# Cross attention and mixture of experts on one core: the mask bias of the scores moved from the score matmuls into the folded key matrix

## The reference, cut to what matters

```python
q = (x @ Wq)...; k = (mem_keys @ Wk)...; v = (mem_values @ Wv)...      # 16 heads of 64
scores = einsum('bhtd,bhsd->bhts', q * inv_temp, k) / sqrt(D)
scores = where(mem_mask, scores, -inf)
# keep the 32 largest of 64 scores of each row and head, softmax over these
out = einsum('bhts,bhsd->bhtd', attn, v) @ Wo
```

## Time and profile before

| what | us |
|---|---|
| median of 3 runs | 1403.3 (1400.73 to 1408.4) |
| the profiled execution | 1396.75 |
| its span, first to last instruction | 1394.9 |
| TensorE busy in the span | 1283.2 (92%) |
| VectorE busy | 942.8 (68%) |
| ScalarE busy | 854.2 (61%) |
| GpSimd busy | 682.3 (49%) |
| mean granted TensorE clock | 0.971 of full |

### The profile page before, as it was taken

How to read it: one execution, slowest core, us unless ns; L and a number is a source line. 1 busy time by engine, 2 the same in 40 slices (tenths; PEclk the granted TensorE clock), 3 DMA queues, 4 the chain that set the end, 5 groups by cost and what they waited for, 6 DMA issues and landing times. The chain is left out here.

```text
span 1394.9 us, 27066 instructions
## 1 busy us (share of the span) xinstructions
PE 1283.2 (92%) x7138; PEld 922.0 (66%) x7138; DVE 942.8 (68%) x6185; ACT 854.2 (61%) x2061; POOL 682.3 (49%) x816
## 2 busy tenths in 40 slices
PE   7868799999999999999999999999972899999996
PEld 5445576577576566656757666655531799989996
DVE  3887987996997998799699789944426122222221
ACT  2334488697878879779787887977860122222221
POOL 2557453555356355445624734632013466666673
PEclk9989999999999999999999999999995899999998
DMA  5210641743363184175337417418513264385551
GB/s 189 83 62 9 167 93 31 169 99 77 101 154 82 55 181 93 40 154 121 77 91 155 91 33 196 78 49 195 93 46 136 77 221 152 82 303 187 188 193 26
DMA packets 105009, 161.43 MB, mean 116 GB/s; under 512 B 35058, under 2 KB 58232, under 8 KB 100760
## 3 DMA queue, kind: packets, MB, share of 16 engines
q1 hardware_dynamic: 86760, 106.51, 32.7%
q0 software_dynamic: 18096, 53.19, 11.7%
HBM read 161.81 MB, written 46.53 MB: 149 GB/s over the span
## 5 line engine op out<-in xcount | busy, mean ns | idle before, releaser
L1013 ACT ACTIVATE pt<-fr 128x512 f32<-128x512 f32 x512 | 277.1, 617 | 25.7 <-PE fr L613 22.6
L1244 DVE CUSTOM_DVE_ANT_0 over<-fr,over 128x256 f32<-128x256 f32 x512 | 197.8, 418 | 86.7 <-ACT over L1023 79.2
L1023 ACT ACTIVATE over<-fr 128x256 f32<-128x256 f32 x512 | 179.0, 391 | 53.4 <-PE fr L613 49.0
L613 PE MATMUL fr<-qs,ks 128*128 128x512 f32 x512 | 189.1, 452 | 3.8 <-DMA qs<-cT 1.3
L613 PE MATMUL fr<-ks,qs 128*128 128x256 f32 x512 | 170.7, 352 | 8.1 <-DVE nmax L1244 3.9
L1358 POOL TENSOR_TENSOR m<-m,e 128x1024 f32<-128x1024 f32 x32 | 75.9, 2371 | 185.0 <-DVE m L1180 185.0
L613 PEld LDWEIGHTS fr<-qs,ks 128*128 128x128 f32 x512 | 87.1, 188 | 86.5 <-issue 50.5
L613 PE MATMUL fr<-kd,qs 128*128 128x256 f32 x512 | 137.5, 283 | 0.0
L814 PE MATMUL ob<-pt,v 128*32 128x512 f32 x1024 | 136.4, 604 | 0.6 <-ACT pt L1013 0.5
L613 PEld LDWEIGHTS fr<-ks,qs 128*128 128x128 f32 x512 | 97.8, 191 | 43.9 <-DVE nmax L1244 25.0
L613 PE MATMUL xs<-VW,pT 128*128 128x256 f32 x512 | 120.2, 389 | 1.8 <-issue 1.7
(11 more groups left out here) (211 smaller groups left out, 2903.9 us busy)
## 6 DMA issues: line engine op xcount, KB each, us to landing
parts_d<-parts SPq DMA_DIRECT2D x32, 512.0 KB, 4.2
ks<-parts_d SPq DMA_DIRECT2D x128, 128.0 KB, 4.0
qs<-parts_d SPq DMA_DIRECT2D x128, 128.0 KB, 4.3
xy_d<-xy SPq DMA_DIRECT2D x32, 256.0 KB, 3.9
kd<-diff_d SPq DMA_DIRECT2D x128, 64.0 KB, 4.1
xyf<-xy_d SPq DMA_DIRECT2D x32, 256.0 KB, 4.0
rows_d<-row SPq DMA_DIRECT2D x32, 256.0 KB, 3.3
diff_d<-diff SPq DMA_DIRECT2D x16, 256.0 KB, 2.3
```

Of the source, the lines that this page charges most:

```text
L613: return pe.matmul(o, l, r, start=first, stop=last)
L1013: act.activation(pt[:, t % 2, h, :], fr_bank(b, "st", 16 * g + n)[:, :], ACT.Exp, scale=D ** -0.5)\
L1023: act.activation(over[:, (16 * g + n + 64 * b) % NREL, :], fr_bank(b, "fs", 16 * g + n)[:, S // 2:S], ACT.Relu)\
L1244: v.tensor_tensor_reduce(rest, fr_bank(b, "fs", 16 * g + n)[:, 0:S // 2], rest, 1.0, -BIG, ALU.add, ALU.max, nmax[:, g % 2, 4 * h + t:4 * ...
```

## The change

The bias matmul of each score half goes, and with it `top` and its memsets. Feature 0 of `xn` is set to one once, by a GpSimd memset of both buffers, and ScalarE writes only features 1 to 255 from then on. Since the normed features add up to zero, the product with feature 0 is minus that of the other 255; the weights of feature 0 are therefore subtracted from those of the others, once, by VectorE (`query_weights`, in two halves of the heads), and set to zero. Row 0 of `M` then holds the bias alone: in `fold_k` the chunks of the first feature half (`mt == 0`) begin with a matmul of one row, `unit[0:1, :]` with the bias, and the products add to it.

```diff
-        top = sa("top", [P, P], F32R)
...
-        blank, top_set, cleared, consts_ready = sem("blank"), sem("top_set"), sem("cleared"), sem("consts_ready")
+        blank, cleared, consts_ready = sem("blank"), sem("cleared"), sem("consts_ready")
+        wq_step, wq_ready, xn_set = sem("wq_step"), sem("wq_ready"), sem("xn_set")
...
-            pe.wait_ge(top_set, 1)
...
                     if b == 0 and c == 0:
-                        pe.wait_ge(wq_loaded, 16)
                         pe.wait_ge(keys_placed, 1)
                     elif c == 0:
                         pe.wait_ge(kbd_loaded, 32 * b)
+                    if b == 0 and c < 2:
+                        pe.wait_ge(wq_ready, c + 1)
                     o = xs_slot(b, "M", c)
                     mt, half = c // 2, c % 2
+                    if mt == 0:
+                        mm(o[:, :].rearrange("p (h c) -> p h c", c=CK), unit[0:1, :],
+                           bias_m[0:1, b * CK:(b + 1) * CK].unsqueeze(1).to_broadcast((1, H // 2, CK)), True, False)
                     for j in range(4):
                         hp = 4 * half + j
-                        ins = mm(o[:, j * P:(j + 1) * P], wqT_s[:, hp, mt * P:(mt + 1) * P], kbd[:, hp, :])
+                        ins = mm(o[:, j * P:(j + 1) * P], wqT_s[:, hp, mt * P:(mt + 1) * P], kbd[:, hp, :], mt > 0, mt > 0 or j == 3)
...
+                if b == 0 and t == 0:
+                    pe.wait_ge(xn_set, 1)
                 pe.wait_ge(xn_ready, b * NT + t + 1)
...
-                    mm(o[:, :].rearrange("p (h c) -> p h c", c=CK), top[:, :],
-                       bias_m[:, b * CK:(b + 1) * CK].unsqueeze(1).to_broadcast((P, H // 2, CK)), True, False)
...
-                        ins = mm(o[:, :], xnT[:, k, :], M[:, k, half * 512:(half + 1) * 512], False, k == KT - 1)
+                        ins = mm(o[:, :], xnT[:, k, :], M[:, k, half * 512:(half + 1) * 512], k == 0, k == KT - 1)
...
-                    copy(xn[:, t % 2, :], x_rows(b)[:, t, :], xr[:, t, 0:1], xr[:, t, 1:2]).then_inc(xn_ready, 1)
+                    copy(xn[:, t % 2, 1:], x_rows(b)[:, t, 1:], xr[:, t, 0:1], xr[:, t, 1:2]).then_inc(xn_ready, 1)
...
+            def query_weights():
+                for part in range(2):
+                    yield due(0, "nh", 0) - 0.02 + 0.015 * part
+                    half = slice(part * HP // 2, (part + 1) * HP // 2)
+                    dve.wait_ge(wq_loaded, 16)
+                    v.tensor_tensor(wqT_s[:, half, 1:], wqT_s[:, half, 1:],
+                                    wqT_s[:, half, 0:1].to_broadcast((P, HP // 2, DM - 1)), ALU.subtract).then_inc(wq_step, 1)
+                    dve.wait_ge(wq_step, part + 1)
+                    v.memset(wqT_s[:, half, 0:1], 0.0).then_inc(wq_ready, 1)
...
-            weave([place_keys()]
+            weave([query_weights(), place_keys()]
...
-            gp.memset(top[:, :].bitcast(F32), 0.0)
+            gp.memset(xn[:, :, 0:1], 1.0).then_inc(xn_set, 1)
             gp.memset(mhalf[:, :], -0.5).then_inc(p_set, 1)
             pool.wait_ge(p_set, 1)
-            gp.memset(top[0:1, :].bitcast(F32), 1.0).then_inc(top_set, 1)
-            pool.wait_ge(top_set, 1)
```

## The result

The changed kernel takes 1416.28 us (median of 9 runs, 1411.48 to 1420.01), the kernel before beside it 1407.52 us (9 runs, 1400.73 to 1409.26): a ratio of 1.0068, with an interval of 1.0048 to 1.0087. It is slower by 9.5 us (the difference of the two means; the medians lie 8.8 us apart), where 1398.3 us was forecast, and the time lies outside the forecast range. Of the 18.0 us of the miss, 4.2 are the median of before itself, which was 1403.3 us over its first 3 runs. The profiled execution has a span of 1414.6 us.

A forecast was written before the change was run, and what follows sets the result against it. In a steady batch TensorE's order sets the pace in one stretch, and either TensorE or VectorE can in the other. Start +0.8 us and six batches -5.8 make -5.0 us, from 1403.3 to 1398.3 us; range 1391 to 1405.5.

The forecast's parts named there:

- the price of the one-row matmul: Two added bias matmuls per batch in the key fold: 0.22 us each, range 0 to 0.36.
- upper end: Added fold matmul: 0.22 us plus up to 0.14 for going to another tile shape and back, 0.36 us.
- The cover that I gave it: Steady batch: the two added matmuls cost half, 0.22 us together, as second-pass matmuls around them partly wait for ScalarE.
- The removal: Steady batch: eight bias matmuls gone from the score halves, of which 0.44 + 0.75 us a batch reaches the end.
- The term of 0.75: Tiles 1 to 3: TensorE's gain shows at VectorE's wait before 510.13 us, at most 0.75 us a batch.
- The waits of tile 0: Two score halves of tile 0, where VectorE waits for TensorE: 0.44 us a batch, kept whole.
- The start: Subtraction delays the fold by 1.45 us, two bias matmuls add 0.6, one removed returns 0.22: first `nhi` 1.8 us later.
- The first two batches: Up to 180 us: 1.8 us late, less 0.44 and 0.6 from removed matmuls, +0.8 us, between -0.6 and +2.6.
- (a): Rival: TensorE is the bound throughout, the whole 7.9 us comes through, 1395.8 us; chance 0.27.
- (d): Rival: more than TensorE's own time, ScalarE's waits for second-pass scores shrink too, 1393.3 us; chance 0.06.
- (b): Rival: VectorE's chain holds the period, nothing but the start is left, 1404.1 us; chance 0.14.
- (c): Rival: late query weights delay the subtraction and push the chain by 2.6 us, 1405.9 us with no steady gain; chance 0.08.

The follow-up runs named there:

- run 2: Changed kernel with the fold's one-row bias matmul made one of 128 rows: ratio 1.0019 to the kernel before, -0.4 us at the same clock.
- run 7: Changed kernel with each one-row matmul issued twice in succession: ratio 1.0076 to the kernel before, +10.8 us at the same clock.
- run 8: Changed kernel with the fold's bias matmul of 32 rows instead of one: ratio 1.0032 to the kernel before, +6.4 us at the same clock.
- run 3: Changed kernel with the fold's 16 bias matmuls left out, so no mask: ratio 0.9984 to the kernel before, -2.3 us at the same clock.
- run 1: Kernel before with its 64 bias matmuls left out, so no mask: ratio 0.9969 to the kernel before, -4.1 us at the same clock.
- run 10: Changed kernel once more, unaltered: ratio 1.0068 to the kernel before, +6.3 us at the same clock.
- run 5: Changed kernel without fold bias matmuls, GpSimd copying the bias into row 0 of M: ratio 1.0031 to the kernel before, +1.6 us at the same clock.
- run 13: Changed kernel, but batch 0 as before, subtraction later, GpSimd writing M's row from batch 1, batch 1's copy behind batch 0 half sums: 1400.58 us, 0.9964 to before.

## Why the prediction was wrong, point by point

**The step that failed is the price of the one-row matmul.** It was taken from the removed matmul, "the same 512 columns: 0.22 us", with 0.36 as the upper end. Measured: 0.61 to 0.62. The row had the columns right and not the rows: 0.22 is the price between neighbours of the same height (runs 2 and 7), and 0.39 more is paid once for each visit (runs 7 and 8). The upper end was worked out from the head outputs (0.99 - 0.86 is 0.13, not 0.14), which differ from their neighbours in columns (128*32), not in rows. They are also not the only other shape in the trace, as the prediction had it: 32 matmuls of `nmax` are listed as 128*16. But these have 128 rows too, so no row of before held a bound. The rule that the prediction put beside it, of the Trainium skill (TensorEngine Tiling (Array Packing), Key Properties), that a change of the tiling mode drains the engine, spoke against the change and agrees with the sign and with runs 7 and 8. The section gives no price, and that a drain is what fills the 0.39 us, no run here shows; the traces show two weight loads that begin only with their own matmul.

**The cover that I gave it was not there.** "I cost at half, since they stand among second-pass matmuls that partly wait for ScalarE": run 3 against the changed kernel gives 1.24 us a batch for two, their whole price. It is all in VectorE's wait for `rz`, 0.25 us without them (before, runs 1 and 3) and 1.46 in the changed kernel.

**The removal was nearly right in the steady stage, in part by luck.** Forecast 0.44 + 0.75 = 1.19 us a batch, measured 0.85 (run 1). The term of 0.75 gave nothing: that wait is 0.75 us in run 1 too. The waits of tile 0 gave 0.56 for 0.44 (0.32 to none, 2.34 to 2.10), and the rest came from places that the sum had left out. From the first tile's `nhi` to the fourth's the changed kernel takes 424.59 - 351.90 = 72.69 us where the kernel before takes 415.38 - 342.32 = 73.06. So a steady batch has -0.85 + 1.24 = +0.39, by the two periods 0.37 us, where -0.97 was forecast: in six batches +2.2 us for -5.8.

**The start: where the fold begins was forecast well, how long it lasts was not.** In the first profile the subtraction begins at 13.53 us for 13.6 and the fold at 16.55 for 16.45. In run 10 the fold begins at 15.74, but its loads landed earlier (VectorE makes `unit`, behind the load of the mask, at 9.88 us, in the trace before at 10.51). From its first matmul to its last end the fold takes 5.3 to 6.3 us in the nine profiles that have no bias matmul in it in batch 0, 8.8 in the first profile and 7.7 in run 10: 3.1 and 1.9 us more than the 5.78 of before, where 0.6 was forecast for the two matmuls. It is the same step again. From there to the first `nhi` run 10 gains 0.2 us, as forecast, and the first profile, with its slow scores, loses 1.5. So run 10's +2.5 us, near the 1.8 that was forecast, is an early landing and a dear fold that partly cancel: luck.

**The first two batches lose more than was forecast.** The 1.0 us that the removal was to give back there is not seen: run 1 gains 4.1 us in all, its six periods alone make 5.1, and its batch 2 begins at 224.49 us for 224.62. With the change batch 2 begins at 230.00 us in run 10 and at 234.72 in the first profile: +5.4 and +10.1 us against the trace before, where +0.8 was forecast. That trace is of a fast execution, so an average one would make the difference smaller; how much of it lies in this stage is open.

**The sum**, at the same clock: -4.1 for the removal (run 1), +1.8 for subtraction and feature 0 (run 3), +8.6 for the 16 matmuls (run 10) make +6.3 us; they add up because they are differences between the same runs. The mean clock of the changed kernel is lower by 0.0024 (run 10), at 0.86 us for 0.001 another 2.0 us; together 8.3 us, which is the difference of the two means there. Why its clock is lower is not settled: run 5, without any bias matmul, has the lowest of all, and run 8, with 16 of them, a higher one than the kernel before beside it.

**The rivals.** (a) and (d) needed a cheap bias, and (a) falls with run 1 besides: of 8 x 0.22 = 1.76 us a batch that TensorE was spared, 0.85 came through. (b), VectorE alone holds the period, falls with the same number: it is half, not nothing. So the weight load's share, one of the two measures that the Trainium skill (Perfetto Trace Analysis, Identifying the Most-Contended Engine) names for TensorE, would have misled here if taken alone. (c) had the right side for the wrong reason: no late weights, but the term that stood in the sum as settled.

## What to carry to other kernels

A matmul's price is read from the starts of its neighbours and holds for its height: one of 1 or 32 rows among those of 128 cost a visit of 0.39 us here besides its columns, so try to fill it up with zero rows (run 2), to put two into one visit (run 7), or to let another engine write the row (run 13). An upper end is a bound only if its row shares what is new in the added operation; here that was the height. And a small copy placed on a queue costs less by its length (1.03 us) than by its wait: look at what stands behind it when its input is late.

## What the runs showed of the hardware that was not expected

The visit of a matmul of 1 or 32 rows: 0.39 us beyond its 0.22, the same for both heights, once for two in succession; on the way in and on the way back a weight load of 0.18 to 0.19 us begins only with its own matmul, where in run 2 it begins 0.23 us ahead. And the mean granted clock of an execution goes with its time, 0.86 us for 0.001 over 268 executions, so that most of the spread between runs of one kernel (0.957 to 0.972, some 13 us) was in that one column, and one profile's start could be 3.6 us later than another's of the same program.
